# Decoder layer in fp32: QKV computed transposed, the rotation done by VectorE out of PSUM, and part of the weight decoding moved to a later stage

## The chip, the cores and the metric

One core of one Trainium2 chip. The metric is the device time of one execution, in microseconds (us). The kernel is one launch and runs a whole decoder layer.

## The reference, cut to what matters

```python
def reference(x, ctx, w_qkv, w_o, Wq, bq, Wk, bk, qweight, lut4, bias):   # x, ctx: (8, 256, 1024) f32
    x = layernorm(x + attention(x, w_qkv, w_o))        # 32 query heads, 8 key/value heads of 32, causal
    x = layernorm(x + cross_attention(x, ctx, Wq, bq, Wk, bk))
    return layernorm(x + ffn(x, qweight, lut4, bias))  # one linear layer with a decoded weight

# attention: q, k, v = split(x @ w_qkv)                # w_qkv: (1024, 1536): 1024 q, 256 k, 256 v columns
#   q and k are rotated: for each head, x1 = even columns, x2 = odd columns,
#   r1 = x1*cos - x2*sin,  r2 = x1*sin + x2*cos, with angles by position and column
#   softmax(q k^T / sqrt(32), causal) v, then @ w_o
# ffn weight: 4 bit planes of 1024 x 1024 bits, packed in int32; the 4-bit code of each weight
#   picks one of 16 values of its row's table (lut4)
```

## The kernel before

Everything is fp32, and every large product is made of three fp32r matmuls: each operand is split into a high part (a rounded copy, made by ScalarE) and a low part (the rest, a subtraction), and hi*hi, hi*lo and lo*hi are added up in one PSUM bank (`product`, lines 569 to 571). The kernel has five stages, one after the other.

**Stage 1 (about 0 to 347 us).** QKV in 16 tiles of 128 tokens. For a tile, TensorE turns x (8 transposes, L578), multiplies with w_qkv in three banks of 512 columns (72 matmuls each) with tokens on the partitions; ScalarE copies each bank to `raw`; VectorE makes the products with the sines (`sines`, L1278), GpSimd those with the cosines (`cosines`, L1684) and the sum (`turned_chunk`, L1692); TensorE turns the rotated tile back (`turn_q`, 10 transposes, L588), ScalarE and VectorE make its parts `qT_hi` and `qT_lo`, and SyncE's queue stores them to `qk_scr` in DRAM. Beside this VectorE decodes the ffn weight, one block of 128 rows for each two tiles, eight blocks in all: `spread` takes 32 shifts of 128x128 (L1291), and a tree of 15 operations on 128x1024 picks the values: 8 `leaf` (L1316, tensor_scalar) and 7 `choose` (L1327, copy_predicated). TensorE turns a finished block (`turn_f`, 8 transposes), its parts are made and `store_f` writes them to `f_scr`.

**Stage 2 (347 to about 789).** Self-attention by batch, 8 units of 4 heads in a batch, each unit in three steps (24 steps k a batch). Units are loaded by SyncE's queue (`load_unit`, seven DMAs). Four slots hold them. The product with w_o for a batch runs beside the next batch's attention; batch 0 has none beside it. What is left of stage 1 (the last tile's third chunk, the last block's last three picks, its turn and its store) is put into the steps of batch 0, w_o is loaded and split there (`WO_STEPS`, k = 14 to 21), and wq is loaded.

**The fold (789 to 897).** M = Wq^T Wk, in 8 row blocks m: `u_row(m)` (16 small matmuls into one bank) and `fold(m)` (48 matmuls of 512 columns). VectorE's round is `u_row` (a copy of 2x128), `m_low` (two subtractions) and `wk_low` of block m+2. TensorE's u_row(m+1) waits for VectorE's copy of u_row(m).

**Stages 4 and 5 (897 to 1387).** Cross-attention in four groups of 512 tokens, then the ffn.

All orders are written out by hand: each engine runs its own list and waits on semaphores.

Of the kernel before, what the change touches and what calls it, by code (L numbers as in the profile page):

```python
# [20 lines left out]

# [11 lines left out]
P = 128  # L33
# [9 lines left out]
RB = ROPE // P  # L43
# [9 lines left out]
PICKS = 15  # L53
ACC_USES = KT + 2 * GT
# [3 lines left out]
def rope_tables():  # L58

    inv = (np.float32(1.0) / np.float32(10000.0) ** (np.arange(0, HD, 2, dtype=np.float32) / np.float32(HD)))  # L60
    ang = np.arange(SEQ, dtype=np.float32)[:, None] * inv.astype(np.float32)[None, :]
    c, s = np.cos(ang).astype(np.float32), np.sin(ang).astype(np.float32)
    one = np.concatenate([np.repeat(c, 2, axis=1), -s, s], axis=1)
    return np.ascontiguousarray(np.stack([one, one * np.float32(-1.0 / math.sqrt(HD))], axis=1).astype(np.float32))


def decoder_layer(nc, x, ctx_in, ctx_cols, w_qkv, w_o, wq, bq, wk, bk, qweight, lut4, bias, rope, out):
# [11 lines left out]
    with top:  # L79
# [38 lines left out]
        u_bc = const("u_bc", [P, D])  # L118
# [3 lines left out]
        w_hi, w_lo, w_in = parts(a1, "w", [P, KT, QKV])  # L122
        x_st = sb("x_st", [P, 2, D])
        qT_hi, qT_lo = sb("qT_hi", [P, RB, P], F32R), sb("qT_lo", [P, RB, P], F32R)
        pick = [sb("pick0", [P, D], I32), sb("pick1", [P, D], I32)]
        raw = sb("raw", [P, ROPE])
        planes = sb("planes", [P, BITS, D // 32], I32)
        lut = sb("lut", [P, LEVELS])
        lut_x = sb("lut_x", [P, LEVELS // 2], I32)
        sb("pad_w", [P, 4 * KT * D - 2 * KT * QKV - 4 * D - 2 * RB * P - ROPE - BITS * D // 32 - LEVELS - LEVELS // 2])  # L130
        for i in range(2):
            sb(f"pad_q3_{i}", [P, REP, SEQ]), sb(f"pad_k3_{i}", [P, SEQ]), sb(f"pad_v_{i}", [P, 2, HD])
        rot_c, rot_s = sb("rot_c", [P, ROPE]), sb("rot_s", [P, ROPE])
        sb("pad_slots", [P, 2 * (REP * SEQ + SEQ + 2 * HD) - 2 * ROPE])
        xT_hi, xT_lo = sb("xT_hi", [P, 2, KT, P], F32R), sb("xT_lo", [P, 2, KT, P], F32R)
        turned = sb("turned", [P, ROPE])
        v_st = sb("v_st", [P, 2, KCOLS])
        tab = sb("tab", [P, 2, 2, 2 * HD])
        bits = sb("bits", [P, BITS, D], I32)
        pick += [sb("pick2", [P, D], I32), sb("pick3", [P, D], I32)]  # L140
        a1.close()
        f_out = [pick[i][:, :].bitcast(F32R) for i in (2, 3)]
# [33 lines left out]
        with nc.sbuf_tensor("b_rows", [P, 2, D], F32) as b_rows:  # L176
# [4 lines left out]
        pc, (pcT_hi, pcT_lo) = sb("pc", [P, 2, SEQ]), [sb(f"pcT_{i}", [P, 2, 2, P], F32R) for i in ("hi", "lo")]  # L181
        nm2, rs2, ri2 = sb("nm2", [P, GT, 2]), sb("rs2", [P, GT]), sb("ri2", [P, GT])
# [17 lines left out]
        w_ld, x_ld = sems("w_ld", KT), sems("x_ld", 2)  # L200
        w_hi_ready, w_lo_ready = sem("w_hi_ready"), sem("w_lo_ready")
        xps_ready, xT_hi_ready, xT_lo_ready = sem("xps_ready"), sem("xT_hi_ready"), sem("xT_lo_ready")
        qkv_done, raw_ready, cos_done, sin_done, turned_ready = (
            sems("qkv_done", 3), sems("raw_ready", 3), sems("cos_done", 3), sems("sin_done", 3), sems("turned_ready", 3))
        qps_ready, qT_hi_ready, qT_lo_ready = sems("qps_ready", 3), sem("qT_hi_ready"), sem("qT_lo_ready")
        qhi_st, qlo_st, v_stored = sem("qhi_st"), sem("qlo_st"), sems("v_stored", 2)
# [46 lines left out]
        CHUNK_BANK = (bank[0], bank[1], bank[2])  # L253
        XPS = (bank[3], bank[4])
        QPS = (bank[5], bank[6], bank[7])
        QBLK = ((0, 4), (4, 8), (8, 10))
        PIECE = (((0, 256, 0), (256, 512, 1)), ((512, 1024, 1),), ((1024, 1280, 1),))
# [19 lines left out]
        Q_TAIL_STEP, F_TAIL_STEP = 2, 8  # L277
        WO_STEPS = {14 + kt: kt for kt in range(KT)}
        WQ_HIGH_STEP, WQ_LOW_STEP = {9: 0, 12: 1}, {10: 0, 13: 1}

# [45 lines left out]
        def _(sp):  # L326

            def load_x(n, slot):
                sp.dma_start(x_st[:, slot, :], xt[bass.ds(n * P, P), :]).then_inc(x_ld[slot], 16)
# [8 lines left out]
            load_x(0, 0)  # L338
            for kt in range(KT):
                rows = w_qkv[kt * P:(kt + 1) * P, :]  # L340
                sp.dma_start(w_in[:, kt, KCOLS:ROPE], rows[:, 0:HEADS * HD]).then_inc(w_ld[kt], 16)
                ends = w_in[:, kt, :].rearrange("p (s c) -> p s c", c=KCOLS)[:, 0:QKV // KCOLS:QKV // KCOLS - 1, :]
                sp.dma_start(ends, rows[:, HEADS * HD:QKV].rearrange("p (s c) -> p s c", c=KCOLS))\
                  .then_inc(w_ld[kt], 16)
                if kt == 1:
                    load_x(1, 1)
            sp.dma_start(tab[:, :, :, :], rope.rearrange("(j p) t c -> p j t c", p=P)).then_inc(tab_ld, 16)
            load_planes(0)
            load_lut(0)
# [3 lines left out]
            sp.wait_ge(xps_ready, 2)  # L353
            load_x(2, 0)

            def store_q(n):

                for i, (t, ready, count, stored) in enumerate(((qT_hi, qT_hi_ready, 3, qhi_st), (qT_lo, qT_lo_ready, 3, qlo_st))):
                    wait_alone(sp, ready, count * n + count)
                    sp.dma_start(qk_scr[i].rearrange("(c p) s -> p c s", p=P)[:, :, bass.ds(n * P, P)],  # L360
                                 t[:, :, :].bitcast(F32)).then_inc(stored, 16)

            def store_f(b):

                sp.wait_ge(f_lo_ready, 2 * b + 2)
                for i in range(2):
                    sp.dma_start(f_scr[i].rearrange("(k p) o -> p k o", p=P)[:, :, bass.ds(b * P, P)],
                                 f_out[i].bitcast(F32).rearrange("p (k o) -> p k o", o=P)).then_inc(f_stored, 16)

            def stage1_batch(b, ahead, first, last):  # L370
                for j in range(2):
                    n = 2 * b + j
                    if not (first and j == 0):
                        store_q(n - 1)
                    if j == 0 and not first:
                        store_f(b - 1)
                        sp.wait_ge(pick_step, PICKS * b)
                        load_lut(b)
                    if j == 1 and not last:
                        sp.wait_ge(codes_ready, 2 * b + 2)  # L380
                        load_planes(b + 1)
                    if ahead[j]:
                        sp.wait_ge(xps_ready, 2 * n + 4)
                        load_x(n + 3, 1 - j)
                    sp.wait_ge(raw_ready[2], n + 1)
                    sp.dma_start(v_scr[bass.ds(n * P, P), :], v_st[:, j, :]).then_inc(v_stored[j], 16)
# [16 lines left out]
            stage1_batch(0, (True, True), True, False)  # L403
# [1408 lines left out]
```

## Time and profile before

| | |
|---|---|
| time, median of 3 runs (range) | 1388.21 us (1386.46 to 1388.99) |
| time of the profiled execution | 1388.76 us |
| its span | 1387.0 us |
| outside of the span | 1.8 us |
| mean granted TensorE clock | 0.971 |
| TensorE busy | 1321.6 us (95%) |
| VectorE busy | 924.8 us (67%) |
| ScalarE / GpSimd busy | 549.7 us (40%) / 543.5 us (39%) |
| DMA | 169.84 MB, 122 GB/s |

Busy times are of the one profiled execution. The durations of matmuls in the profile overlap, because they are pipelined: what one costs in a stream is read from the distance between two starts, and so are VectorE's operations in a row. The granted clock is a share of 2.4 GHz; 0.5 is 1.2 GHz.

### The profile page before, as it was taken

The page shows a single profiled execution, that of the slowest core. Times are in us where ns is not written, and L with a number is a line of the kernel's source. Part 1 is how long each engine was busy: PE and PEld are TensorE (multiplying, and loading weights), DVE is VectorE, ACT ScalarE, POOL GpSimd, SP SyncE. Part 2 cuts the span into 40 slices and gives each one's busy share as a digit, 9 for nine tenths or more (in the row PEclk, how much of TensorE's full clock was granted, in tenths as well). Part 3 has the DMA queues.
Part 4 walks back from the last instruction along what each step waited for, and adds up shares of the span by engine and source line. Part 5 has one row for each costly group of instructions (what it writes and reads, how often), then busy time and mean ns, then how long its engine had stood idle before and what let it go on. Part 6 is the DMA issues. An engine that isn't in the chain of part 4 may idle for free.

```text
span 1387.0 us, 25843 instructions
## 1 busy us (share of the span) xinstructions
PE 1321.6 (95%) x8086; PEld 1070.3 (77%) x8086; DVE 924.8 (67%) x2558; ACT 549.7 (40%) x1633; POOL 543.5 (39%) x467
## 2 busy tenths in 40 slices
PE   7799999999679999999999999999999999999998
PEld 6687777787557777777777778788888888788886
DVE  6988888988787888887888422225353534666665
ACT  4222222222677777877777211224242423200000
POOL 1534343434545565556556100043544442222221
PEclk9899999999769999999999999999999999999999
DMA  7334334334793444434343421202424154522222
GB/s 252 91 116 142 120 116 127 96 119 134 223 260 92 128 117 128 129 116 141 117 125 106 159 84 46 76 1 77 167 77 167 62 182 183 203 88 86 83 86 76
DMA packets 161916, 169.84 MB, mean 122 GB/s; under 512 B 35520, under 2 KB 136128, under 8 KB 161856
## 3 DMA queue, kind: packets, MB, share of 16 engines
q1 hardware_dynamic: 161856, 169.07, 38.4%
q8 instruction: 33, 0.54, 0.2%
q14 instruction: 27, 0.22, 0.1%
HBM read 112.40 MB, written 56.62 MB: 122 GB/s over the span
## 4 chain that ended last, share of the span: by engine, by line
PE 67%; issue 13%; DVE 12%; POOL 3%; ACT 1%; SPq 1%; DMA 1%; DVEq 0%; POOLq 0%; ACTq 0%
PE bank L727 13%; PE bank L569 12%; PE bank L571 12%; PE bank L570 12%; PE bank L673 7%; DVE pick L1327 5%; PE bank L660 4%; POOL x2b L1790 3%; PE bank L700 2%; DVE pick L1316 2%; PE bank L704 2%; DVE rot_s L1278 2%; PE bank L578 1%; PE bank L837 1%; DVE qT_lo L1241 1%
## 5 line engine op out<-in xcount | busy, mean ns | idle before, releaser
L1718 POOL TENSOR_TENSOR prob<-prob,rinv 128x512 f32<-128x512 f32 x192 | 206.7, 1077 | 174.8 <-DVE rinv L1386 174.5
L1038 ACT ACTIVATE prob<-bank,nmax 128x256 f32<-128x256 f32 (+1 forms) x512 | 211.3, 427 | 98.1 <-DVE nmax L1378 88.5
L1378 DVE CUSTOM_DVE_ANT_0 bank<-bank,mask 128x256 f32<-128x256 f32 (+1 forms) x512 | 168.8, 380 | 6.2 <-PE bank L660 3.5
L569 PE MATMUL bank<-w_hi,xT_hi 128*128 128x512 f32 x384 | 157.4, 410 | 4.1 <-DVE w_lo L1241 4.1
L571 PE MATMUL bank<-w_hi,xT_lo 128*128 128x512 f32 x384 | 152.7, 398 | 0.0
L570 PE MATMUL bank<-w_lo,xT_hi 128*128 128x512 f32 x384 | 152.2, 396 | 0.0
L1684 POOL TENSOR_TENSOR rot_c<-raw,tab 128x256 f32<-128x256 f32 (+1 forms) x64 | 83.7, 1317 | 166.1 <-ACT raw L969 126.4
L673 PE MATMUL bank<-ident,prob 128*128 128x128 f32 x768 | 129.3, 294 | 8.8 <-POOL prob L1718 8.4
L673 PEld LDWEIGHTS bank<-ident,prob 128*128 128x128 f32 x768 | 89.8, 147 | 44.4 <-issue 18.6
L660 PE MATMUL bank<-k,q 96*128 96x256 f32 (+1 forms) x512 | 108.6, 317 | 7.0 <-DMA vv<-v_scr 5.6
L969 ACT ACTIVATE raw<-bank 128x512 f32<-128x512 f32 (+1 forms) x48 | 25.3, 527 | 221.9 <-PE bank L571 221.7
L1038 ACT ACTIVATION_READ_ACCUMULATOR prob<-bank,nmax 128x1 f32 x512 | 107.8, 210 | 0.0
L727 PE MATMUL bank<-wo_hi,att_hi 128*128 128x512 f32 x256 | 104.4, 408 | 0.0
L1533 DVE SCALAR_TENSOR_TENSOR k_lo<-bank,bA,k_hi 128x512 fp32r<-128x512 f32 x32 | 24.0, 751 | 120.2 <-ACT k_hi L1142 114.7
L569 PE MATMUL bank<-cT_hi,m_hi 128*128 128x512 f32 x256 | 101.1, 395 | 0.7 <-issue 0.7
L569 PE MATMUL bank<-f_hi,x2T_hi 128*128 128x512 f32 x256 | 101.0, 394 | 0.8 <-DVE x2T_lo L1241 0.8
L727 PE MATMUL bank<-wo_hi,att_lo 128*128 128x512 f32 x256 | 101.6, 397 | 0.0
L727 PE MATMUL bank<-wo_lo,att_hi 128*128 128x512 f32 x256 | 101.0, 395 | 0.0
L571 PE MATMUL bank<-cT_hi,m_lo 128*128 128x512 f32 x256 | 100.4, 392 | 0.0
L570 PE MATMUL bank<-cT_lo,m_hi 128*128 128x512 f32 x256 | 100.4, 392 | 0.0
L571 PE MATMUL bank<-f_hi,x2T_lo 128*128 128x512 f32 x256 | 99.8, 390 | 0.0
L570 PE MATMUL bank<-f_lo,x2T_hi 128*128 128x512 f32 x256 | 99.7, 389 | 0.0
(158 smaller groups left out, 3053.3 us busy)
## 6 DMA issues: line engine op xcount, KB each, us to landing
q<-qk_scr SPq DMA_DIRECT2D x192, 128.0 KB, 2.4
x_st<-x_scr SPq DMA_DIRECT2D x32, 512.0 KB, 4.0
qk_scr<-qT_hi SPq DMA_DIRECT2D x16, 640.0 KB, 3.8
qk_scr<-qT_lo SPq DMA_DIRECT2D x16, 640.0 KB, 3.9
x_st<-x SPq DMA_DIRECT2D x16, 512.0 KB, 3.4
f_scr<-pick SPq DMA_DIRECT2D x16, 512.0 KB, 5.1
y<-x SPq DMA_DIRECT2D x16, 512.0 KB, 3.5
x_scr<-y SPq DMA_DIRECT2D x16, 512.0 KB, 2.8
```

The source lines that it names most:

```text
L569: nc.tensor.matmul(o, l_hi, r_hi, start=first, stop=False)
L570: nc.tensor.matmul(o, l_hi, r_lo, start=False, stop=False)
L571: return nc.tensor.matmul(o, l_lo, r_hi, start=False, stop=last)
L660: mm = nc.tensor.matmul(o[:, i * keys:(i + 1) * keys], q3[slot][:, h, t0:t0 + P], k3[slot][:, 0:keys], start=i == 0, stop=i == len(hs) - 1 ...
L673: mm = nc.tensor.transpose(tb[:, at * P:(at + 1) * P], prob[:, k % 4, c:c + P], ident[:, :])
L727: mm = nc.tensor.matmul(o[:, :], lt[:, kt, st * P:(st + 1) * P], rt[:, kt, half * BANK:(half + 1) * BANK], start=kt == 0 and ps == 0, stop ...
L1038: mm = nc.scalar.activation(prob[:, k % 4, i * keys:(i + 1) * keys], SBANK[pos][:, i * keys:(i + 1) * keys], ACT.Exp, bias=nmax[:, k % 4, ...
L1327: nc.vector.copy_predicated(o[:, :], bits[:, bit, :], other[:, :]).then_inc(pick_step, 1)
L1378: mm = nc.vector.tensor_tensor_reduce(part, part, mask[:, 2 * P - keys:2 * P], 1.0, BIGGEST, ALU.add, ALU.min, nmax[:, k % 4, i:i + 1])
L1684: mm = nc.gpsimd.tensor_tensor(head(rot_c), head(raw), cs, ALU.mult)
L1718: nc.gpsimd.tensor_tensor(pr, pr, rinv[:, k % 4, 0:n].unsqueeze(2).to_broadcast([P, n, keys]), ALU.mult)\
L1790: nc.gpsimd.tensor_tensor(x2b[:, j, :], x2_st[:, j, :], bias_bc[:, :], ALU.add).then_inc(x2b_ready, 1)
```

## The change

- **QKV transposed.** x comes in already transposed from the host (`x_cols`), and w_qkv with its columns sorted (`qkv_columns`): for each of 5 chunks of 256 columns (a *pair*) first the 128 even, then the 128 odd columns of the heads; the sixth chunk is v. The work goes by four groups g of 512 tokens. A turn (g, c) with c = 0 to 4 is `qk_pair`: 48 matmuls of 512 columns with the weights as the stationary operand, even half in one bank, odd half in another. Turn (g, 5) is `values`: 96 matmuls of 256 columns.
- **Rotation on VectorE out of PSUM.** `rope_pair`: six tensor_tensor operations on 128x512; two of the four products are written back to PSUM in place. No transposes of x and of the rotated q and k, no `raw`.
- **Low parts on GpSimd.** ScalarE copies the high parts of a pair (`rope_high`), GpSimd subtracts (`rope_low`, two of 128x512) as soon as they are there, and SyncE stores the pair with four DMAs. GpSimd also makes the low parts of w for chunks 2 to 5.
- **Decoding.** Six of the eight blocks are decoded in stage 1, in 24 parts (`spread` as one part, the tree as three of 5 operations), one part a turn, two in turn (1, 2), none in (3, 5). A block is turned one turn after its last part (`F_TURN`). Blocks 6 and 7 are decoded in the fold, by `LATE_PARTS` one part at m = 1, two at m = 2, 3 and 4, one at m = 5, and turned after fold(4) and fold(6).
- **Loads.** Units 0 to 2 of batch 0 are loaded after group 0. Half of w_o is loaded in the last group, half right after it. The loads of wq are spread between those of units 6, 7, and batch 1's first two. The loads of x1 in the fold come after those of wk.

```diff
+            def rope_pair(g, c):
+                n = PAIRS * g + c
+                slot, ty = n % 2, 0 if c == PAIRS - 1 else 2
+                dve.wait_ge(a_done, n + 1)
+                wait(dve, r_stored[slot], 64 * (n // 2))
+                even, odd = PAIR_BANK[slot]
...
+                times(rot[:, slot, 0, :], even, 0).then_inc(a_turned, 1)
+                times(even[:, :], even, 1)
+                dve.wait_ge(b_done, n + 1)
+                times(rot[:, slot, 2, :], odd, 0)
+                times(odd[:, :], odd, 1).then_inc(b_turned, 1)
+                dve.wait_ge(b_turned, n + 1)
+                nc.vector.tensor_tensor(rot[:, slot, 0, :], rot[:, slot, 0, :], odd[:, :], ALU.subtract)
+                nc.vector.tensor_tensor(rot[:, slot, 2, :], rot[:, slot, 2, :], even[:, :], ALU.add).then_inc(r_ready, 1)
...
+            for g, c in ORDER:                                   # VectorE
+                if c < PAIRS:
+                    rope_pair(g, c)
+                if (g, c) in F_TURN:
+                    f_low(F_TURN[g, c])
+                if c == PAIRS and g < GROUPS - 1:
+                    for kt in range(KT):
+                        x_low(g + 1, kt)
+                for part in PARTS[PART_END[g, c] - PARTS_OF[g, c]:PART_END[g, c]]:
+                    for go in part:
+                        go()
...
+            def qk_pair(g, c):                                   # TensorE
+                n = PAIRS * g + c
+                wait(pe, r_ready, n - 1)
+                for kt in range(KT):
...
+                    if c == 0:
+                        pe.wait_ge(x_lo_ready, KT * g + kt + 1)
+                    for half in range(2):
+                        cols = slice(half * P, (half + 1) * P)
+                        mm = product(PAIR_BANK[n % 2][half][:, :], w_hi[:, c, kt, cols], w_lo[:, c, kt, cols],
+                                     x_hi[:, kt, :], x_lo[:, kt, :], kt == 0, kt == KT - 1)
+                        if kt == KT - 1:
+                            mm.then_inc((a_done, b_done)[half], 1)
...
+            for at in ORDER:
+                if at[1] < PAIRS:
+                    qk_pair(*at)
+                else:
+                    values(at[0])
...
+                if at in F_TURN:
+                    turn_f(F_TURN[at])
...
+            for g, c in ORDER:                                   # ScalarE
+                if c < PAIRS:
+                    rope_high(g, c)
+                else:
+                    if g < GROUPS - 1:
+                        for kt in range(KT):
+                            x_high(g + 1, kt)
+                    values_out(g)
+                if g == 0 and c < 3:
+                    w_high(c + 3)
+                if (g, c) in F_TURN:
+                    f_high(F_TURN[g, c])
...
+            w_low(2)                                             # GpSimd
+            w_low(3)
+            for g, c in ORDER:
+                if c < PAIRS:
+                    rope_low(g, c)
+                if g == 0 and c < 2:
+                    w_low(c + 4)
...
+            decode_late(1)                                       # VectorE, fold
+            for m in range(2, KT):
+                u_row(m)
+                m_low(m, m % 2)
+                if m < KT - 2:
+                    wk_low(m + 2, m % 2)
+                if m in F_FOLD:
+                    f_low(F_FOLD[m], LATE_FBANK)
+                decode_late(m)
```

## Rows read from the trace of the kernel before

**Rows 1.** The page: span and the two busiest engines (busy us, share, instructions).

```profile
span 1387.0 us, 25843 instructions
PE 1321.6 (95%) x8086; PEld 1070.3 (77%) x8086; DVE 924.8 (67%) x2558; ACT 549.7 (40%) x1633; POOL 543.5 (39%) x467
```

**Rows 2.** Busy time by stage: length, busy us of each engine, granted clock, DMA share, GB/s.

```profile
0.00:20.00 20.00, 11.38 (x42) 9.27 (x43) 10.18 (x7) 11.32 (x9) 1.65 (x11) 1.00 0.93 340
20.00:347.00 327.00, 301.96 (x1452) 250.26 (x1451) 288.62 (x597) 75.17 (x155) 136.31 (x110) 0.97 0.40 118
347.00:412.00 65.00, 44.52 (x344) 34.74 (x342) 51.33 (x192) 45.86 (x161) 30.86 (x26) 0.67 0.87 250
789.00:897.00 108.00, 108.00 (x568) 84.86 (x566) 26.46 (x42) 18.79 (x28) 0.55 (x1) 0.99 0.20 65
```

**Rows 3.** TensorE's groups of instructions, 20 to 347: busy, mean ns | idle before, releaser.

```profile
L569 PE MATMUL bank<-w_hi,xT_hi 128*128 128x512 f32 x373 | 152.3, 408 | 0.0
...
L588 PE MATMUL bank<-ident,turned 128*128 128x128 f32 x156 | 25.5, 278 | 4.9 <-POOL turned L1692 4.9
...
L578 PE MATMUL bank<-ident,pick 128*128 128x128 f32 x56 | 10.0, 337 | 20.1 <-DVE pick L1327 20.1
```

**Rows 4.** Timeline of TensorE, start and duration: first matmuls, 512-column and 256-column streams.

```profile
10.56 0.77 PE L569 MATMUL bank<-w_hi,xT_hi 128*128 128x512 f32 x1 [4.08 <-DVE w_lo L1241]
...
12.40 0.63 PE L570 MATMUL bank<-w_lo,xT_hi 128*128 128x512 f32 x1
...
826.43 0.39 PE L569 MATMUL bank<-wq_hi,wk_hi 128*128 128x512 f32 x1
...
828.02 0.39 PE L570 MATMUL bank<-wq_lo,wk_hi 128*128 128x512 f32 x1
...
945.39 0.28 PE L569 MATMUL bank<-k_hi,x1T_hi 128*128 128x256 f32 x1
...
947.78 0.28 PE L571 MATMUL bank<-k_hi,x1T_lo 128*128 128x256 f32 x1
```

**Rows 5.** VectorE's groups of instructions, 20 to 347, shapes apart.

```profile
L1327 DVE COPY_PREDICATED pick<-bits,pick 128x1024 int32<-128x1024 int32 x52 | 75.2, 1447 | 4.6
...
L1291 DVE TENSOR_SCALAR bits<-planes 128x128 int32<-128x128 int32 x256 | 39.2, 301 | 0.0
...
L1278 DVE TENSOR_TENSOR rot_s<-raw,tab 128x256 f32<-128x256 f32 x32 | 19.7, 657 | 18.2 <-ACT raw L969 18.2
```

**Rows 6.** Timeline of VectorE and GpSimd, single operations (start, duration).

```profile
75.74 0.68 DVE L1241 TENSOR_TENSOR qT_lo<-bank,qT_hi 128x512 fp32r<-128x512 f32 x1
76.34 1.27 DVE L1241 TENSOR_TENSOR xT_lo<-bank,xT_hi 128x512 fp32r<-128x512 f32 x2
...
85.52 0.81 DVE L1316 TENSOR_SCALAR pick<-bits,lut_x,lut 128x1024 int32<-128x1024 int32 x1
```

**Rows 7.** Timeline near 338 us: a GpSimd operation and the pick beside it.

```profile
338.18 1.29 POOL L1692 TENSOR_TENSOR turned<-rot_c,rot_s 128x512 f32<-128x512 f32 x1 [0.49 <-POOL rot_c L1684]
...
338.30 1.72 DVE L1316 TENSOR_SCALAR pick<-bits,lut_x,lut 128x1024 int32<-128x1024 int32 x1
```

**Rows 8.** Timeline of SyncE's queue: one of the seven issues of a unit's load.

```profile
352.94 0.42 SPq L395 DMA_DIRECT2D q<-qk_scr  x1
```

**Rows 9.** Timeline at stage 2's head: first scores, outputs of units 0 and 4.

```profile
347.22 1.21 PE L660 MATMUL bank<-k,q 96*128 96x256 f32 x8
...
367.36 0.41 DVE L1403 COPY att<-bank 128x256 f32<-128x256 f32 x1
...
398.86 0.41 DVE L1403 COPY att<-bank 128x256 f32<-128x256 f32 x1
```

**Rows 10.** Timeline of the fold: end of fold(2), and VectorE's round behind it.

```profile
832.84 0.60 ACT L969 ACTIVATE m_hi<-bank 128x512 f32 x1 [4.84 <-PE bank L571]
...
838.29 1.22 DVE L1241 TENSOR_TENSOR wk_lo<-wk_in,wk_hi 128x1024 fp32r<-128x1024 f32 x1 [4.00 <-ACT wk_hi L969]
...
844.76 0.60 ACT L969 ACTIVATE m_hi<-bank 128x512 f32 x1 [4.84 <-PE bank L571]
```

More of the change, by code:

```diff
@@ L22 @@
+import itertools
 import math
@@ L813, in _ @@
             fold(1, 1)
-            with pe.Fori(1, KT // 2) as m2:
-                for slot in range(2):
-                    u_row(2 * m2 + slot, slot)
-                    fold(2 * m2 + slot, slot)
+            for m in range(2, KT):
+                u_row(m, m % 2)
+                fold(m, m % 2)
+                if m in F_FOLD:
+                    turn_f(F_FOLD[m], LATE_FBANK)
+            pe.wait_ge(f_lo_ready, 2 * BATCH)
             pe.wait_ge(bA_ready, 2)
@@ new lines, in x_high, with w_high, rope_high @@
+            def x_high(g, kt):
+                act.wait_ge(xw_ld[kt], 16 * (g + 2))
+                copy(x_hi[:, kt, :], x_in[:, kt, :]).then_inc(x_hi_ready, 1)
+            def w_high(c):
+                act.wait_ge(w_ld[c - 1], 16)
+                for h in range(2):
+                    flat = lambda w: w[:, c, 4 * h:4 * h + 4, :].rearrange("p k s -> p (k s)")
+                    copy(flat(w_hi), flat(w_in)).then_inc(w_hi_ready, 1)
+            def rope_high(g, c):
+                n = PAIRS * g + c
+                slot = n % 2
+                act.wait_ge(r_ready, n + 1)
+                copy(rot[:, slot, 1, :].bitcast(F32R), rot[:, slot, 0, :])
+                copy(rot[:, slot, 3, :].bitcast(F32R), rot[:, slot, 2, :]).then_inc(r_hi_ready, 1)
@@ new lines, in values_out @@
+            def values_out(g):
+                act.wait_ge(x_used, KT * (g + 1))
+                for j in range(2):
+                    wait(act, v_stored, 16 * (2 * g + j))
+                    copy(v_st[:, :, :].rearrange("p t c -> p (t c)"), VBANK[j][:, :]).then_inc(v_copied, 1)
+            for kt in range(KT):
+                act.wait_ge(xw_ld[kt], 32)
+                copy(w_hi[:, 0, kt, :], w_in[:, 0, kt, :]).then_inc(w_hi_ready, 1)
+                x_high(0, kt)
+            w_high(1)
@@ L1358, in _ @@
+            PARTS = [part for b in range(EARLY) for part in decode(b)]
             dve.wait_ge(consts_step, 4)
-            x_low(0, 0)
             for kt in range(KT):
                 dve.wait_ge(w_hi_ready, kt + 1)
-                low(w_lo[:, kt, :], w_in[:, kt, :], w_hi[:, kt, :]).then_inc(w_lo_ready, 1)
-            x_low(1, 1)
-            dve.wait_ge(tab_ld, 16)
-            stage1_batch(0, True, False)
-            with dve.Fori(1, BATCH - 1) as b:
-                stage1_batch(b, False, False)
@@ L1371, in maxima @@
+            for slot in range(2):
+                dve.wait_ge(r_stored[slot], 64 * PAIRS * GROUPS // 2)
             def maxima(b, k):
```

541 lines of the change are left out of this document (232 added, 309 removed).

## The prediction

> **What bounds the kernel now.** I read the page first, then the busy times by stage, then TensorE's and VectorE's groups in stage 1, and last the timelines. The page says that TensorE is busy for 95% and VectorE for 67% of 1387.0 us [rows 1]. An average hides that the stages differ. In stage 1 TensorE shows 302 and VectorE 289 of 327 us, at a granted clock of 0.97; in the head of stage 2 the clock is 0.67 and TensorE shows 45 of 65; in the fold TensorE is busy throughout and VectorE for 26 of 108 us [rows 2]. So stage 1 has two engines close to full, and what either saves counts only as far as the other follows. In it TensorE makes 1152 product matmuls of 512 columns and turns x, the rotated tile and the blocks; it waits 20.1 us for the last pick of seven blocks and 4.9 us for GpSimd's sums [rows 3].
>
> What a matmul costs is a distance of starts [rows 4]. 512 columns: 1.59 us over 7 steps, 0.227 us. 256 columns: 2.39 over 20, 0.120. The first ones run at 1.2 GHz: 1.84 over 4, 0.46. A transpose lasts 0.278 on the mean [rows 3], like a 256-column matmul [rows 4], so I take nearly that one's step, 0.11.
>
> **TensorE's new stage 1.** Removed: 160 + 128 transposes, some 31 us. The columns stay. A pair is 48 x 0.227 = 10.9 us, a values turn 96 x 0.120 = 11.5, a `turn_f` 8 x 0.11 = 0.9. When is the first pair done? The first matmul starts at 10.6 [rows 4] behind 1.3 MB; the new first k-step needs 0.4 MB, which at the 340 GB/s of the first 20 us [rows 2] takes 1.2 us a step. I take 6 us for the first start (an estimate: some 4 for the first loads, 2 for the splits), 10.9 for the pair and 2 for its beginning at 1.2 GHz: 18.8. Behind it come 19 pairs (207), 4 values turns (46) and 6 `turn_f` (5): 258 us, if nothing is waited for.
>
> **VectorE's new stage 1.** A rotation is six tensor_tensor of 128x512. The nearest row reads one operand from PSUM and one from SBUF with GpSimd at work beside it, and steps by 0.60 us (75.74 to 76.34) [rows 6]. Six are 3.6; with the wait in the middle and at the start 3.9. The other bound: the old sine product, both operands in SBUF and strided, 0.657 for 256 elements [rows 5], 1.31 for 512; four of those and two of 0.60 make 6.4. The new products are dense and read one tile in PSUM, so I take 3.9. Twice PSUM is also the output; no row shows that.
>
> A block's decoding: `spread` is 32 x 0.153 = 4.9; 7 `choose` of 1.45 [rows 5]; 8 `leaf` of 0.81 alone [rows 6]. With 0.1 for each semaphore wait the four parts are 5.0, 5.0, 6.3 and 6.3, 22.6 a block. But `leaf` is slower beside GpSimd: 1.72 instead of 0.81 when an operation of 1.29 had begun just before it [rows 7]. `rope_low` is two such operations a pair, 2.6 us, starting about 1.3 us behind each rotation, at the part's head. Bounds for what they cost a part: nothing, and all 2.6. By where the leaves lie in the parts I take 1.9, 0.7, 0.9 and 0.2, 3.7 a block: 26.3.
>
> The sum: 20 rotations 78; 6 blocks 158; 24 `x_low` of 0.60, 14; 12 `f_low`, 8; and in each of six turns VectorE waits some 1.9 for `f_high`, which ScalarE makes only behind `rope_high`, 11. Together 269 us against TensorE's 258. **VectorE becomes the bound of stage 1, narrowly**: 18.8 + 269 = 288.
>
> Where TensorE pays: at each `turn_f` (needs the last pick) and each new group (needs `x_low`). Within a group the turns balance, 3.9 + 6.6 = 10.5 against 10.9. Turn (1, 2) has two parts and an `f_low`; VectorE is then 5 to 6 us late, the next two turns give none back, `turn_f(2)` waits for it in turn (1, 5), and there ScalarE makes all `x_high` and `values_out` before `f_high`, and VectorE `f_low` before `x_low`. I expect 7 to 8 us of idle TensorE there and 4 in all other places. 18.8 + 258 + 12 = 289, the same end.
>
> Two small terms: GpSimd splits w (8 operations of 1024 columns, about 2.6 each) beside the first group's decoding, +2; and stretches at 1.2 GHz after the waits (now 0.97 over stage 1), +3. First scores at 294 instead of 347: **-53 us**.
>
> A rule of the Trainium skill bears on GpSimd's part. First the row: the pick next to GpSimd's sum lasted until about 0.55 us after its end, while the `qT_lo` step stayed at 0.60 [rows 6, 7]. "SBUF — State Buffer", section "Who interferes with whom", says that GpSimd and VectorE share a port pair which whoever comes first keeps for the whole instruction, and that a VectorE instruction with at most one SBUF input outside the two-port modes does not contend. By that the rotation is free of GpSimd (the trace agrees), while every leaf that starts inside `rope_low` waits for its end.
>
> **SyncE.** An issue takes 0.42 [rows 8]. The pair stores (four issues), the x loads and three early units (21 issues, some 10 us) sit in one queue. A slot of `rot` comes free some 9 us after its rotation (an estimate: 1.3 for the high parts, 2.6 for the low ones, 1.7 for four issues, 3 to land) and is wanted again 18 us after (two turns of 10.9 less the rotation). Early units are waited for at the end of group 0 only. I price this at nothing; if the cover went it would be some 5 us, once.
>
> **Head of stage 2.** Before: the first scores start at 347.2, unit 0 is out 20 us later, unit 4 at 399 [rows 9]. VectorE has three picks, a rest of the rotation and a block's parts in between, and DMA is at 0.87 [rows 2] with 4 MB of w_o, 4 MB of wq and the block's store. After, these picks are gone, and half of w_o is already there. Units 5 to 7, in whose steps w_o is split, I leave as they are. From the first scores to unit 4 it takes 52 us now, 8 for each unit behind the first. TensorE's 45 busy us in 65 at 0.67 of its clock [rows 2] don't let a unit go much below 6.5, so I take 15 for unit 0 and 6.5 to 7 for each of the next four: 42. **-10**; bounds: 0 (the low clock makes the pace) and -18.
>
> **The fold.** Now fold to fold is 844.76 - 832.84 = 11.9 us [rows 10]. VectorE's round: `wk_low` starts 5.5 behind the end of fold(m), behind its load, and ends at 6.7 [rows 10]; I take 6.1, as its load now comes earlier. The parts are queued behind it. Two are 11.3 without GpSimd (5.0 + 6.3), so the round ends 17.4 after fold(m), and only then comes the copy that TensorE's next-but-one `u_row` waits for, due at 11.9: 5.5 us of idle TensorE behind m = 2. Walking on with VectorE's round of 14 to 17: 2.2 behind m = 3, 4.6 behind m = 4 (`f_low` in it), nothing behind m = 1, 5, 6. With two `turn_f` (1.8): 14; with one of clock, **+15**. Bounds: +2 (if it all hid) and +25. VectorE's 26 of 108 busy us [rows 2] look like room for 45 us of picks; the round's order is why it isn't.
>
> **The sum.** 1388.8 (the profiled execution, 1387.0 of span and 1.8 around it) - 53 - 10 + 15 = 1340.8. The median of the runs is 0.6 lower: **1340**.
>
> **Rivals.**
> - *GpSimd holds VectorE in full*, in every part: 24 parts at +2.6 instead of +0.9 mean, +40 on VectorE's sum, less the 6 that the turns' slack takes: stage 1 ends some 35 later, 1375; half of it, 1357. For it: [rows 7]. Against: that row is of a leaf; a `choose` has a mean of 1.45 with GpSimd's work in it [rows 5]. This is where the port rule of the Trainium skill ("SBUF — State Buffer", same section) would lead if every operation of the decoding came behind GpSimd.
> - *The fold hides the decoding*: TensorE loses only the turns, 1327. For it: VectorE is idle for three quarters there. Against: the order of the round.
> - *The rotation costs more than the transposes saved*: from 3.9 to 6.4 us a pair stage 1 ends 46 later (20 x 2.5, less slack), 1386. From 6.5 us a pair on, 1.1 an operation, the kernel is slower than before; at 6.8, 1394. For it: PSUM as output in place is unseen. Against: [rows 6].
> - *Stage 2's head gains nothing*, the low clock sets its pace: 1350.
>
> **Chances.** The forecast (1332 to 1349) 0.5; GpSimd's hold, in half or full, 0.2; the fold hidden or the head faster 0.17; no gain in the head 0.08; rotation at the old price 0.05. The range 1320 to 1364 leaves out the full hold and the dear rotation. Within 0.2% is what a measurement of this kernel cannot tell from no change. Faster 0.94, within 0.2% 0.02, slower 0.04: only the dear rotation, or the full hold with another wait, ends there.
>
> **What would show it.** First scores near 294; six operations of a rotation in 3.9; TensorE's idle time before L578 of blocks and before the matmuls of c = 0, most of it near the end of group 1; `leaf` between 0.8 and 1.7; unit 4 out 42 us behind the first scores; in the fold idle time before the `u_row` matmuls behind m = 2, 3 and 4, 12 us in sum. The prediction is wrong if a rotation takes over 4.5 us, if the pair store or x's load is what a wait ends on, or if TensorE waits nowhere in the fold.

## The result, and the profile after

The changed kernel takes 1354.22 us (median of 4 runs, 1353.77 to 1356.42), against 1388.2 of the kernel before beside it: ratio 0.976, 95% interval 0.9743 to 0.9777. That is 34 us less, where 48 less were forecast; 1340 was the forecast, 1320 to 1364 its range. The profiled execution took 1353.77 us, 1352.0 of it span. The page of the changed kernel (beside [rows 1]):

```profile
span 1352.0 us, 24745 instructions
PE 1285.0 (95%) x7990; PEld 1047.6 (77%) x7990; DVE 928.9 (69%) x2504; ACT 529.0 (39%) x1579; POOL 491.4 (36%) x403
```

Its busy times by stage, with the columns of [rows 2] and the stages where they now lie: start, stage 1, head of stage 2, fold.

```profile
0.00:20.00 20.00, 14.31 (x55) 11.61 (x56) 11.75 (x20) 10.89 (x20) 1.65 (x11) 1.00 0.91 322
20.00:304.00 284.00, 262.75 (x1340) 224.09 (x1338) 258.46 (x441) 53.92 (x89) 88.21 (x48) 0.96 0.43 141
304.00:364.00 60.00, 41.07 (x335) 32.41 (x334) 44.09 (x182) 45.89 (x160) 27.09 (x24) 0.69 0.77 232
739.50:863.20 123.70, 112.68 (x584) 89.27 (x582) 67.67 (x142) 21.46 (x34) 0.55 (x1) 0.96 0.24 74
```

TensorE's timeline has the marks: the end of the wait for block 0's picks, the first scores (`k,q` matmuls, eight for a unit), the first matmul after them, the first scores of unit 4, the first w_o matmul.

```profile
74.55 1.75 PE L632 MATMUL bank<-ident,pick 128*128 128x128 f32 x7 [10.65 <-DVE pick L1370]
...
303.94 1.11 PE L700 MATMUL bank<-k,q 96*128 96x256 f32 x8
312.88 0.77 PE L700 MATMUL bank<-k,q 96*128 96x256 f32 x2 [7.83 <-ACT prob L1078]
...
329.85 0.50 PE L700 MATMUL bank<-k,q 96*128 96x256 f32 x2 [2.10 <-DMA vv<-v_scr]
...
363.78 0.73 PE L771 MATMUL bank<-wo_hi,att_hi 128*128 128x512 f32 x1
```

VectorE's timeline has the outputs of units 0 and 4:

```profile
322.74 0.41 DVE L1437 COPY att<-bank 128x256 f32<-128x256 f32 x1
...
349.67 0.41 DVE L1437 COPY att<-bank 128x256 f32<-128x256 f32 x1
```

The first scores come at 303.9 instead of 347.2 [rows 9], 43.3 us earlier. The fold starts at 739.5 instead of 789.3, so stage 2 gives 6.5 us more, nearly all of it in its head. The keys start at 863.2 instead of 897.7: the fold gives 15.3 us back. -43.3 - 6.5 + 15.3 = -34.5; the spans differ by 35.0. The forecast had -53 - 10 + 15.

What TensorE waited for, up to 320 us (sum, times, longest), and in the fold:

```profile
PE bank L632 <- DVE pick L1370: 16.4, 4, 10.7
PE bank L623 <- DVE xc_lo L1279: 9.4, 2, 5.7
PE bank L700 <- ACT prob L1078: 7.8, 1, 7.8
PE bank L623 <- DVE rot L1320: 1.0, 1, 1.0
...
PE bank L834 <- DVE b_rows L1518: 10.3, 3, 5.3
```

Of the 9.4 us for x's low parts 5.7 are the wait before the very first matmul, which the forecast has in its 18.8. Behind the first pair, from 19.0 us to the first scores, the busy times are:

```profile
18.98:303.94 284.96, 263.71 (x1344) 224.89 (x1342) 259.48 (x443) 54.02 (x89) 88.21 (x48) 0.96 0.43 142
```

TensorE waits there for VectorE for 21.1 us (16.4 + 3.7 + 1.0), where the forecast has 14 (12, and 2 for w's splits), and it is busy for 263.7 us at a clock of 0.96, where the forecast has 261 (258, and 3 for stretches at 1.2 GHz). The 7 and the 3 us are those by which the first scores miss 294. The largest single wait, 10.7 us, lies in the first group, where the forecast had next to none. At the end of group 1 it is 4.7 and 3.7, 8.4 us, for the 7 to 8 forecast. VectorE's and GpSimd's timelines in the first group:

```profile
22.70 14.01 DVE L1331 TENSOR_SCALAR bits<-planes 128x128 int32<-128x128 int32 x32
...
43.41 5.53 DVE L1359 TENSOR_SCALAR pick<-bits,lut_x,lut 128x1024 int32<-128x1024 int32 x2
...
55.51 5.54 DVE L1359 TENSOR_SCALAR pick<-bits,lut_x,lut 128x1024 int32<-128x1024 int32 x2
```

```profile
21.05 9.48 POOL L1716 TENSOR_TENSOR w_lo<-w_in,w_hi 128x1024 fp32r<-128x1024 f32 x4 [18.55 <-ACT w_hi L1010]
...
42.64 5.75 POOL L1716 TENSOR_TENSOR w_lo<-w_in,w_hi 128x1024 fp32r<-128x1024 f32 x2 [9.61 <-ACT w_hi L1010]
...
54.88 5.63 POOL L1716 TENSOR_TENSOR w_lo<-w_in,w_hi 128x1024 fp32r<-128x1024 f32 x2 [3.54 <-ACT w_hi L1010]
```

Read the two together: `spread`, 32 short operations, takes 14.0 us beside `w_low` and `rope_low` (4.5 in the fold, where GpSimd makes no sums), and each pair of `leaf` beside `w_low` 5.5; alone a pair takes 1.53 (at 40.3 us). The groups of the decoding in stage 1 (0 to 305) show the sum over all six blocks, with GpSimd's operations below:

```profile
L1370 DVE COPY_PREDICATED pick<-bits,pick 128x1024 int32<-128x1024 int32 x42 | 76.2, 1814 | 3.7
L1359 DVE TENSOR_SCALAR pick<-bits,lut_x,lut 128x1024 int32<-128x1024 int32 x48 | 50.5, 1092 | 0.5
L1331 DVE TENSOR_SCALAR bits<-planes 128x128 int32<-128x128 int32 x192 | 39.6, 366 | 0.0
...
L1725 POOL TENSOR_TENSOR rot<-rot 128x512 f32<-128x512 f32 x20 | 41.2, 2060 | 0.0
L1724 POOL TENSOR_TENSOR rot<-rot 128x512 f32<-128x512 f32 x20 | 27.1, 1354 | 177.9 <-ACT rot L1010 177.9
L1716 POOL TENSOR_TENSOR w_lo<-w_in,w_hi 128x1024 fp32r<-128x1024 f32 x8 | 20.9, 2634 | 31.7 <-ACT w_hi L1010 31.7
```

VectorE's three rows are `choose`, `leaf` and `spread`; they add up to 166.3 us. `choose`, the forecast's "1.45", is now 1.81 on the mean. The second operation of `rope_low` is 2.06 where the first is 1.35: GpSimd is held too.

The third wait is new, 7.8 us right behind the first scores. Its cause stands on the timelines of SyncE's queue, ScalarE and VectorE:

```profile
303.06 0.34 SPq L367 DMA_DIRECT2D lut<-lut  x1
303.44 1.90 SPq L389 DMA_DIRECT2D qk_scr<-rot  x4
305.38 0.56 SPq L394 DMA_DIRECT2D v_scr<-v_st  x1
```

```profile
308.42 0.60 ACT L1010 ACTIVATE v_st<-bank 128x512 f32<-128x512 f32 x1 [4.60 <-DMA v_scr<-v_st]
308.91 1.08 ACT L1010 ACTIVATE pick<-bank 128x512 fp32r<-128x512 f32 x2
```

```profile
309.53 1.29 DVE L1279 TENSOR_TENSOR pick<-bank,pick 128x512 fp32r<-128x512 f32 x2 [6.50 <-ACT pick L1010]
310.74 0.42 DVE L1412 CUSTOM_DVE_ANT_0 bank<-bank,mask 128x256 f32<-128x256 f32 x1
```

`v_st` is one buffer. The second half of the values must wait until the first is stored; that store stands in SyncE's queue behind a table's load, which waits for the last pick, and behind the last pair's four issues. `f_high` is queued behind the copy on ScalarE, `f_low` behind `f_high` on VectorE, and the first `maxima` of stage 2 behind `f_low`. The same store holds ScalarE for 3.2 us at the end of group 1.

### The profile page after: what moved, and what is told of

It is laid out like the page before. It is cut to its first block, busy times and chain, and to the rows that moved or that the text cites. A ratio compares the mean times of both kernels' runs of the same rounds, so it can differ in the third digit from the quotient of the medians.

```text
span 1352.0 us, 24745 instructions
## 1 busy us (share of the span) xinstructions
PE 1285.0 (95%) x7990; PEld 1047.6 (77%) x7990; DVE 928.9 (69%) x2504; ACT 529.0 (39%) x1579; POOL 491.4 (36%) x403
## 4 chain that ended last, share of the span: by engine, by line
PE 63%; DVE 15%; issue 13%; POOL 4%; DMA 2%; ACT 2%; SPq 1%; POOLq 0%; DVEq 0%; ACTq 0%
PE bank L771 13%; PE bank L623 10%; PE bank L625 10%; PE bank L624 10%; PE bank L715 7%; DVE pick L1370 4%; PE bank L700 4%; POOL x2b L1817 3%; PE bank L742 2%; DVE pick L1359 2%; PE bank L672 2%; PE bank L746 2%; DVE bits L1331 1%; DVE rot L1310 1%; DVE bank L1310 1%
## 5 line engine op out<-in xcount | busy, mean ns | idle before, releaser
L623 PE MATMUL bank<-xc_hi,w_hi 128*128 128x512 f32 x320 | 126.7, 396 | 10.5 <-DVE xc_lo L1279 9.4
L624 PE MATMUL bank<-xc_lo,w_hi 128*128 128x512 f32 x320 | 125.9, 394 | 0.0
L625 PE MATMUL bank<-xc_hi,w_lo 128*128 128x512 f32 x320 | 125.7, 393 | 0.0
L700 PE MATMUL bank<-k,q 96*128 96x256 f32 (+1 forms) x512 | 107.4, 314 | 10.2 <-ACT prob L1078 8.1
L1010 ACT ACTIVATE rot<-rot 128x512 fp32r<-128x512 f32 x40 | 23.1, 625 | 201.6 <-DVE rot L1320 201.6
L1724 POOL TENSOR_TENSOR rot<-rot 128x512 f32<-128x512 f32 x20 | 27.1, 1354 | 177.9 <-ACT rot L1010 177.9
```

Source lines behind the costliest of these rows:

```text
L623: nc.tensor.matmul(o, l_hi, r_hi, start=first, stop=False)
L624: nc.tensor.matmul(o, l_hi, r_lo, start=False, stop=False)
L625: return nc.tensor.matmul(o, l_lo, r_hi, start=False, stop=last)
L700: mm = nc.tensor.matmul(o[:, i * keys:(i + 1) * keys], q3[slot][:, h, t0:t0 + P], k3[slot][:, 0:keys], start=i == 0, stop=i == len(hs) - 1 ...
L1724: nc.gpsimd.tensor_tensor(tile(0), tile(0), tile(1), ALU.subtract)
```

## Experiments

Times are medians on the chip. The changed kernel is 0.976 of the kernel before (0.9743 to 0.9777); the others' ratios are beside them with their intervals. Those of 2, 3, 4, 6 and 10 overlap with it, and those of 1 and 5 touch it at the edge; there the traces' marks decide. The kernel before, which ran beside each batch of experiments, had medians from 1384.7 to 1388.2 us, so differences of times from two batches (7 and 8 against the changed kernel, 11 against 8) are uncertain by up to some 3.5 us.

**1. The order in the fold.**

```
+            u_row(2)
             decode_late(1)
             for m in range(2, KT):
-                u_row(m)
                 m_low(m, m % 2)
                 ... wk_low, f_low ...
+                if m < KT - 1:
+                    u_row(m + 1)
                 decode_late(m)
```

> In the fold VectorE copies the next u_row before the decode parts instead of behind them; its amount of work stays. Theory (the order of VectorE's round makes TensorE wait): the three waits of TensorE before its u_row matmuls, 10.3 us in the changed kernel, go to under 1 us, and the time falls from 1354 to about 1344. Rival (VectorE simply has too much to do there, or wk's loads come late): the waits move to the matmuls that need wk_lo, and the time stays at 1351 to 1355.

1346.53 us, 0.9716 (0.9685 to 0.9747). TensorE's waits in the fold:

```profile
PE bank L632 <- DVE late_a L1370: 3.9, 2, 2.2
```

The 10.3 us before `u_row` are gone altogether, with the same work on VectorE. 3.9 us have come in for the last picks of the two late blocks, which until then hid behind them. The fold takes 116.2 us (740.0 to 856.2) instead of 123.7. The first scores (304.3) and the head are as before. The order was the cause. The next waits, 3.9, are the amount's, or so it seemed (experiment 12).

**2. w's low parts on VectorE.**

```
 GpSimd:  -  w_low(2), w_low(3), and w_low(c + 4) in the first group
 VectorE: +  behind rope_pair(0, c), c < 4: two low() of chunk c + 2
```

> w's low parts of pairs 2 to 4 and of the values are made by VectorE, each behind a rotation of the first group, not by GpSimd beside the decoding; VectorE gets 8 operations more, about 9 us. Theory (GpSimd's long splits held VectorE's decoding, about 18 us in the first group): spread of block 0 falls from 14.0 us to under 5.5, TensorE's wait of 10.7 us before block 0's transposes falls to under 4, and the time falls from 1354 to 1346 or a little below. Rival (VectorE has too much work in the first group, whoever runs beside it): the wait stays or grows by up to 9, 1354 to 1362.

1355.74 us, 0.9783 (0.9755 to 0.9811): no gain. The wait before block 0's transposes is 8.4 us, not under 4, and first scores come at 302.3. `spread` of block 0 takes 6.7 us, and the six blocks' decoding 154.1 instead of 166.3: 12 us saved and 9.4 spent. With GpSimd free, `rope_low` starts on time, 1.3 us behind the rotation (at 24.3 in the first turn), where before it had run late behind `w_low` (30.5). The theory missed the size of the gain; whether the hold of `w_low` counts was open until experiments 7 and 8.

**3. GpSimd's sums beside the next rotation.** This takes back one piece of the change: that GpSimd subtracts as soon as the high parts are there.

```
                 pool.wait_ge(r_hi_ready, n + 1)
+                if n < PAIRS * GROUPS - 1:
+                    pool.wait_ge(a_turned, n + 2)
```

> GpSimd makes a pair's low parts only when VectorE has begun its next rotation (but for the last pair), so that they run beside the rotation and not at the head of a decode part. Theory (GpSimd's sums hold the decoding, by some 1.8 us a part, and not the rotation): choose beside GpSimd falls from 2.3 to 1.4 us, a rotation stays at 3.7 us, and first scores come 6 to 12 us before the 303.9 of the changed kernel: 1342 to 1348. Rival (a rotation is held too, or its slot comes back too late from its store): the gain on the parts is given back, 1352 to 1365, with the wait to be seen before the rotation's first product.

1351.07 us, 0.9754 (0.9725 to 0.9783). The decoding takes 138.9 us instead of 166.3, and a product of a rotation 0.69 as before, so the sums hold the parts and not the rotation. But first scores come only 2.8 us earlier, at 301.1, and the time lies between the theory's range and the rival's. The waits of VectorE and of TensorE from 78 to 172 us say where the rest went:

```profile
DVE pick L1279 <- ACT pick L1010: 11.1, 2, 9.4
DVE rot L1310 <- DMA qk_scr<-rot: 4.1, 1, 4.1
```

```profile
PE bank L623 <- DVE xc_lo L1279: 10.2, 1, 10.2
```

**4. The block's high part before the values, the pair's store before the table.**

```
 ScalarE, c == PAIRS:   x_high(g + 1, ...); + f_high if due; values_out(g)
 SyncE, last group:     + store_pair(g, PAIRS - 1) ahead of decode_loads((g, PAIRS - 1))
```

Other than the expectation says, the values' store stays behind the table's load; only the pair's store is moved.

> At a group's end ScalarE makes a turned block's high part before it copies the values out, and at the end of the last group SyncE's queue has the store of the last pair and of the values before the load of the next table. Theory (in the head of stage 2 TensorE's 7.8 us of idle time behind the first scores is the round trip of the values' store through one buffer): that idle time falls to about 3 us (the high parts, low parts, maximum, exponent and scaling must still follow one another), VectorE's wait at the end of the second group falls by 2 or 3 too, and the time falls from 1354 to about 1348. Rival (the low clock and the unit loads make the pace of the head): unit 4 is out at the same time as before from the start of the span, and the time stays at 1352 to 1355.

1355.09 us, 0.9781 (0.9747 to 0.9814): no gain, and yet the wait fell as the theory said, from 7.8 to 4.2 us (about 3 expected), with unit 0 out 14.8 us behind the first scores instead of 18.8. It was given back at once. TensorE's timeline:

```profile
308.52 0.76 PE L700 MATMUL bank<-k,q 96*128 96x256 f32 x2 [4.15 <-ACT prob L1080]
...
330.71 0.80 PE L700 MATMUL bank<-k,q 96*128 96x256 f32 x2 [7.68 <-DMA vv<-v_scr]
```

That is unit 4's load: the scores of units 0 to 3 are eight matmuls each, and this is the next. Its last part was issued at 320.4 and landed 10.3 us later, behind four loads of w_o (2 MB), which SyncE issues just ahead of it. In the changed kernel TensorE waits 2.1 us for it. The first w_o matmul is at 365.3 us, 62.0 behind the first scores.

**5. No low parts of q and k.** GpSimd subtracts 8 columns only; the low parts of q and k are left out.

> GpSimd leaves out the subtraction that makes the low parts of q and k (it subtracts 8 columns of one tile only), so its work beside VectorE in stage 1 is gone but for w's splits. Theory (the hold of the parts is a real cost on the way to the first scores): 6 to 12 us faster than the changed kernel, 1342 to 1348, and as fast as the kernel with late low parts to within 2 us. Rival (VectorE's lost time there is slack, and TensorE or its clock sets stage 1): within 2 us of 1354.

1346.43 us, 0.9716 (0.9688 to 0.9744), first scores at 296.9: 7.0 us of stage 1 hang on GpSimd's sums as the kernel stands. The kernel with late sums gets 2.8 of them and is 4.6 us slower than this one, not within 2; the slot that comes back late takes some of the rest.

**6. Unit loads spread over three turns**, on top of experiment 3.

```
 SyncE:  -  load_unit(0, 0..2) together behind group 0
         +  load_unit(0, c) behind store_pair(1, c), c < 3
```

> As the kernel with late low parts, but the 21 issues that load the first three units stand in SyncE's queue behind the stores of pairs 0, 1 and 2 of the second group, seven at a time, and not together ahead of them. Theory (the late low parts' gain was given back because a pair's store stood behind the units' issues and VectorE's rotation waited 4.1 us for it, which made TensorE wait 10.2 us for x's low parts at the end of the second group): the wait of the rotation is gone, TensorE's wait there falls to about 6, and first scores come at 297 instead of 301: 1344 to 1347. Rival (the wait for x's low parts has its own cause, the order of the high parts at a group's end): first scores stay at 300 to 301 and the time at 1348 to 1351.

1350.24 us, 0.9747 (0.9719 to 0.9775), first scores at 299.3. VectorE's wait for the pair's store is gone, but TensorE's 10.2 us for x's low parts are still there. The slot was worth 1.8 us (301.1 to 299.3), and the rival has the rest: the waits for x's low parts have their own cause, the order at the group's end, where VectorE waits 9.3 us for `f_high` though x's high parts are made before it.

**7 and 8. All together, without and with w's low parts on VectorE.** Edits 1, 3, 4 and 6, and at a group's end VectorE's `x_low` before `f_low`; the second adds edit 2.

> Together: u_row copied ahead of the decode parts, low parts of q and k beside VectorE's next rotation, unit loads spread, block's high part before the values' copies, the last pair's store ahead of the table's load, and x's low parts before the block's at a group's end. Theory (the causes are separate and their gains add, 8 in the fold, 5 to 7 in stage 1, 3 to 6 at the head and the group's end): 1333 to 1338. Rival (they share one slack, so that TensorE's waits move from one to the other): 1340 to 1344.

> All of the last one, and w's low parts of pairs 2 to 4 and of the values on VectorE behind the rotations of the first group. Theory: with GpSimd's sums of q and k no longer beside the decoding, VectorE now keeps the 17 us that the splits cost it less the 9 that it must spend on them, so TensorE's wait before block 0's transposes shrinks by up to 8 and the time is 2 to 6 us below that of the last one. Rival (GpSimd's splits beside the decoding cost nothing that counts): equal to it within 2 us, or above.

1328.49 us, 0.9598 (0.9574 to 0.9622), and 1318.15 us, 0.9522 (0.9497 to 0.9547). Alone the edits had given 8 (1), 4 (3 with 6) and nothing (4, 2); the order of `x_low` gives 4 (experiment 10). Together without edit 2 it is 26 us by the medians and 22 by the ratios, for a sum of 16, and below what either theory or rival had. Edit 2, which gained nothing alone, is now worth 10. First scores come at 287.6 and 279.2; the marks say the same as the times, 16.3 us earlier with all but edit 2, where one by one it was 4.6 (3 with 6), 4.9 (10) and 0.7 (4). In the last kernel the decoding shows what it costs with no GpSimd beside it:

```profile
L1370 DVE COPY_PREDICATED pick<-bits,pick 128x1024 int32<-128x1024 int32 x42 | 60.1, 1431 | 3.7
L1359 DVE TENSOR_SCALAR pick<-bits,lut_x,lut 128x1024 int32<-128x1024 int32 x48 | 36.8, 810 | 0.5
L1331 DVE TENSOR_SCALAR bits<-planes 128x128 int32<-128x128 int32 x192 | 27.0, 310 | 0.0
```

123.9 us, 42.4 less than in the changed kernel.

**9. Unit 3 first**, on top of 8.

```
 SyncE, last group, ahead of store_pair(g, PAIRS - 1):
+    sp.wait_ge(r_ready, PAIRS * GROUPS)
+    load_unit(0, 3, False)
```

> As the kernel with all edits (1318), but the load of unit 3 is issued as soon as the last rotation is done, ahead of the last pair's store, the values' store and the block's store, and not behind them. Theory (in the head of stage 2 TensorE waits for the load of unit 3, 3.5 us there and 7.7 us in the kernel with the high part first, which is where that kernel's gain of 4 us at the first scores was given back): that wait is gone, the first w_o matmul comes 3 us earlier behind the first scores, and the time is 1314 to 1316. Rival (the low clock and the chain of maximum, exponent and scaling make the pace): the wait moves to the next units and the time stays at 1317 to 1319.

1314.92 us, 0.949 (0.947 to 0.9509), whose interval overlaps with that of 8; the marks decide. TensorE's wait for a load (3.5 us in 8) is gone, and from the first scores (279.0) to the first w_o matmul (333.3) it is 54.4 us, where 8 had 58.3 and the changed kernel 59.8. Unit 4 is out 40.3 us behind the first scores. The clock in that stretch did not rise (first line 8, second line 9):

```profile
279.00:338.00 59.00, 41.25 (x338) 32.75 (x337) 44.58 (x184) 46.22 (x161) 27.10 (x24) 0.73 0.77 219
279.00:333.00 54.00, 38.86 (x333) 30.64 (x331) 43.69 (x181) 45.31 (x161) 27.09 (x24) 0.72 0.77 236
```

So waits, not the clock alone, had set the head's pace. But the theory named the wrong load. The wait in 8 stands before the scores of unit 4, not of unit 3. SyncE's queue and the time from issue to landing of the last part of unit 4's load (issues at 292.7 to 296), first in 8, then in 9:

```profile
290.47 1.90 SPq L432 DMA_DIRECT2D wo_in<-w_o  x4
...
295.76 0.43 SPq L427 DMA_DIRECT2D vv<-v_scr  x1
...
vv<-v_scr SPq DMA_DIRECT2D x1, 32.0 KB, 7.2
```

```profile
284.84 3.75 SPq L432 DMA_DIRECT2D wo_in<-w_o  x4
...
295.82 0.43 SPq L427 DMA_DIRECT2D vv<-v_scr  x1
...
vv<-v_scr SPq DMA_DIRECT2D x1, 32.0 KB, 3.3
```

Unit 4's load is issued at the same time in both, but lands 3.9 us earlier in 9, where unit 3's seven issues no longer stand ahead of w_o's four and w_o's 2 MB start 5.6 us earlier. That w_o's bytes are what it had to wait for is the likely reading; no run moves w_o alone.

**10. x's low parts first**, alone on the changed kernel.

```
 VectorE, c == PAIRS:  x_low(g + 1, ...) for all kt, then f_low if due (before: f_low first)
```

> The changed kernel with one edit: at a group's end VectorE makes the low parts of x for the next group before those of the turned block. Theory (the order at a group's end costs TensorE its wait for x's low parts): TensorE's two waits for x's low parts fall from 9.4 to about 5 us and the time from 1354 to about 1350. Rival (VectorE is behind anyway, and the wait moves to the next block's picks): 1353 to 1355.

1350.33 us, 0.9735 (0.9714 to 0.9755), first scores at 299.0. TensorE's waits for x's low parts fall from 9.4 to 5.7 us, and those 5.7 are the start of the kernel: the 3.7 at the end of group 1 are gone, and nothing took their place.

**11. Everything of 8, but the sums at once.**

> All edits of the kernel at 1318 but one: GpSimd makes the low parts of q and k at once, beside the decoding, as in the changed kernel. Theory (each part of the decoding loses 1.8 us to GpSimd, 24 parts some 40 us of VectorE's time, and with the other waits gone stage 1 has slack for about half of it): first scores come 12 to 20 us later than 279 and the time is 1330 to 1338. Rival (delaying the low parts gains only the 3 us that it gained alone): 1320 to 1323.

1335.90 us, 0.964 (0.9623 to 0.9657), first scores at 296.4: 17 us later than in 8, and the time 18 higher. By the ratios the difference is 16. This is the price of subtracting at once when nothing hides it; alone it had shown 3. The decoding:

```profile
L1370 DVE COPY_PREDICATED pick<-bits,pick 128x1024 int32<-128x1024 int32 x42 | 75.4, 1795 | 3.7
L1359 DVE TENSOR_SCALAR pick<-bits,lut_x,lut 128x1024 int32<-128x1024 int32 x48 | 46.3, 1006 | 0.5
L1331 DVE TENSOR_SCALAR bits<-planes 128x128 int32<-128x128 int32 x192 | 32.3, 328 | 0.0
```

It takes 154.0 us, so `rope_low` holds it by 30.1 (154.0 - 123.9), 1.25 a part, not the 1.8 of the expectation; what follows for the time is as the theory had it.

**12. The late parts as 2, 2, 2, 2**, on top of 9.

```
-LATE_PARTS = {1: 1, 2: 2, 3: 2, 4: 2, 5: 1}
+LATE_PARTS = {1: 2, 2: 2, 3: 2, 4: 2}
 SyncE: the last block's table is loaded at m == 4, not 5
```

> As the kernel with unit 3 early (1314.9), but in the fold the eight parts of the last two blocks' decoding stand as 2, 2, 2, 2 behind m = 1 to 4, not as 1, 2, 2, 2, 1 behind m = 1 to 5, with the table of the last block loaded one step earlier. Theory (the 4.0 us that TensorE still waits for the last pick before each of the two late blocks' transposes come from picks that end just behind the fold they are due after): both waits are gone, 1311 to 1313. Rival (VectorE's round of two parts is then too long in each of four folds in a row, and TensorE waits for wk's low parts or for u_row instead): 1314 to 1320.

1313.42 us, 0.9475 (0.9452 to 0.9498): not to be told from 9. Both waits for picks in the fold are gone, as the theory said, and part of the rival came true with it:

```profile
PE bank L832 <- DVE b_rows L1523: 2.6, 2, 1.9
```

The fold is 114.4 us long, against 113.8 in 9. Of the 15.3 us that the fold had lost, some 5 or 6 stay: the two `turn_f`, and small waits that move but don't go.

## Why the prediction came out as it did

**Right: stage 1's two sides, the rotation, the fold.** The first matmul starts at 5.7 us (6 forecast). Six operations of a rotation take 3.7 us (3.9 forecast), whether GpSimd is at work or not, and the products that go back to PSUM in place cost what the others do (0.69 and 0.68), so the rival of the dear rotation fell. TensorE's own side (18.8 + 258 = 277) is what experiment 9 reaches: 279.0. From 19.0 us to the first scores VectorE is busy for 259.5 us; the forecast's sum is 269 with 11 us of waits in it and without w's splits, so 260 to compare. That they agree is in part luck: six blocks without GpSimd are 123.9 us (experiment 8), where the forecast has 136 (22.6 a block), 6 of them for semaphore waits, and what GpSimd adds was forecast too low by more than that. The fold lost 15.3 us for 15: waits of 0.3, 4.7 and 5.3 us before `u_row`, 10.3 in sum for 12.3, and nothing where 2.2 were due; the turns and the clock (0.96 for 0.99 [rows 2]) made up the difference. Experiment 1 showed that VectorE's order is the cause of the waits.

**Mis-sized: what GpSimd costs the decoding.** This is the term that was furthest off, and the waits that it feeds are 7 of the 10 us by which stage 1 missed; the other 3 are TensorE's own work at the clock of 0.96. The forecast had 3.7 a block for `rope_low`, 22 us, and "+2" for w's splits: 24. Measured, it is 42.4: 30.1 from `rope_low` (11 against 8), and 15.0 from `w_low` (3, 138.9, against 8, 123.9), which overlap a little in the changed kernel. Of the 42.4, `choose` has 16.1 (76.2 - 60.1), `leaf` 13.7 and `spread` 12.6. Two things were wrong. `choose` was taken to be free of GpSimd, from its mean of 1.45 in [rows 5]; it takes 1.81 now, and 1.43 where no sum runs beside it. And w's splits were priced as eight operations that delay each other a little, when they were long ones beside the first three parts, one behind the other: 20.9 us of them cost VectorE 15. The Trainium skill ("SBUF — State Buffer", section "Who interferes with whom") says that a VectorE instruction with two SBUF inputs contends with a GpSimd instruction that reads SBUF. `choose` is one. By that rule it belonged to the price; the traces agree with the rule, 1.81 against 1.43. The forecast applied the section's rules to the rotation, where they held, and to the leaves, and not to `choose`.

The way into the time was as forecast: VectorE late, and TensorE waiting at `turn_f`. But the place was another: 10.7 of the 21.1 us lie at the end of the first group, where the splits are, with the clock at 0.74 from 60 to 80 us. The rival "GpSimd holds VectorE" is true in half: 1.25 us a part from `rope_low` and, with w's splits, 1.8 a part (42.4 over 24), halfway between the 0.9 forecast and the 2.6 of the full hold. The measured 1354 is nearer to that rival's 1357 than to 1340, and outside the 1332 to 1349 that had the chance of 0.5. The 18 us more than forecast were partly offset by the base that was 12 too high; how much of either reached TensorE no run separates.

**Right: the end of group 1,** 8.4 us for 7 to 8, though with a cause that was not in the sum: beside the order of `f_high` and `f_low`, `values_out` waits 3.2 us for a store. Experiment 10 took away the order of VectorE's queue there alone: first scores 4.9 us earlier, 299.0 for 303.9.

**Mis-sized: the head of stage 2**, -10 forecast, -6.5 measured, unit 4 out 45.7 us behind the first scores for 42. It is unit 0 that is late, 18.8 us for 15; the four units behind it take 26.9, 6.7 each, as forecast. The queue's price was put at nothing for stage 1 and not looked at where stage 1 ends. There the values' store is part of a wait of 7.8 us (4.1 of it stay when the block's high part no longer stands behind it), and unit 4's load, issued behind 2 MB of w_o, costs 2.1. Taking the first away alone gave nothing (4); both away, unit 0 is out after 15.2 and unit 4 after 40.3 (9).

**Why single edits gained so little.** TensorE's path goes from VectorE through ScalarE or SyncE's queue and back, with several waits due at nearly the same time. Taking away one shows the next. 27 us less of decoding on VectorE brought the first scores 3 us forward alone (3); 30 less brought them 17 forward with the other waits gone (11 against 8). That the edits do more together than the sum of their single gains is measured; which pair of them shares which wait was not separated further than here.

The best kernel, 12, is 73 us faster than the kernel before and about 40 faster than the changed one, with 9 as good.

## What to carry to other kernels

Before work goes to GpSimd, list what VectorE runs beside it, instruction by instruction, and ask of each whether it stays at its price; here one half of VectorE's work (the rotation) did and the other half (the decoding) did not. An operation that is moved to an in-order queue is priced by what is queued behind it: two of the waits here went away or shrank by order alone (u_row behind the picks, `f_high` behind the second copy to `v_st`), and a third (unit 4's load) when other loads were issued in another order ahead of it. Before such a wait is given a cause, count which load it is: here it was the next unit's, not the one that was suspected. And an experiment that takes away one suspect and gains nothing has not cleared it: read in the trace whether its own wait is gone and which took its place, and try it again with that one gone.

## What the runs showed of the hardware

- A product of VectorE with its input and its output in the same PSUM bank costs what one with its output in SBUF does: 0.69 us each for 128x512, 0.60 from start to start.
- The hold goes both ways. Beside `choose` GpSimd's own 1.29 us became 2.3 to 2.4, while `choose` went from 1.39 to 2.3.
- A row of 32 short operations is held much as long ones are: `spread` took 14.0 us with 10.4 us of GpSimd's operations beside it and 4.5 alone, a pair of `leaf` 5.5 with 5.0 beside it and 1.53 alone.
- A load of 32 KB, issued 3 to 5 us behind 2 MB of other loads in the same queue, landed after 7.2 us; with these issued 5.6 us earlier, after 3.3 (experiments 8 and 9).
